# First phase of a gated expert block: each group of TensorE products is signalled by a Drain behind it in place of its last product

## The reference, cut to what matters

```
cf = sigmoid(fft2(n).real.mean(pixels) @ W.T + b)      # one factor per image and channel
sf = fft2(n.mean(channels)).real                       # one factor per image and pixel
x  = x + n * cf + n * sf                               # first half: "x1"
t  = tokens of x                                       # 16384 tokens of 64 channels
g  = layernorm(t) ; p = softmax(g @ gate_w + gate_b)   # 8 experts
e  = argmax(p) ; rank = running count of tokens sent to e
y  = (relu(g @ w1[e] + b1[e]) @ w2[e] + b2[e]) * p[e]  if rank < 2560 else 0
out = x + y, back as images
```

## Time and profile before

| | us |
|---|---|
| median of three executions | 496.19 |
| the profiled execution | 491.18 |
| its span | 488.8 |
| first phase, to the last indirect DMA of L445 | 0 to 262.6 |
| second phase | to 459 |

### The profile page before, as it was taken

The page is one execution under the profiler, slowest core; times in us unless marked ns, Lnnn a source line. Parts: engine busy times, 40 slices in busy tenths (PEclk is TensorE's granted clock), DMA queues, the critical chain, the costliest instruction groups (busy, mean ns, idle before and its releaser), DMA issues.

```text
span 488.8 us, 5544 instructions
## 1 busy us (share of the span) xinstructions
PE 278.9 (57%) x1574; PEld 197.2 (40%) x1574; DVE 248.2 (51%) x694; ACT 160.7 (33%) x301; POOL 227.0 (46%) x234
## 2 busy tenths in 40 slices
PE   7695645857191753614004888927477370839562
PEld 5584544846181653504001444514243130415251
DVE  4588366494554836645100367924445161527943
ACT  2362504342150513203000666714254051435300
POOL 0004727317366372757677335374726657461300
PEclk9666656576566665656555999986979586767967
DMA  7991010203000000000003513302113130100089
GB/s 242 413 380 49 29 51 26 60 7 97 11 11 13 4 15 5 15 12 12 13 14 79 105 28 69 82 24 66 44 29 72 40 68 24 34 19 4 7 312 375
DMA packets 38056, 36.16 MB, mean 74 GB/s; under 512 B 27995, under 2 KB 30620, under 8 KB 38034
## 3 DMA queue, kind: packets, MB, share of 16 engines
q1 hardware_dynamic: 29474, 25.71, 17.3%
q0 software_dynamic: 7264, 5.87, 4.2%
q10 hardware_dynamic: 1296, 4.33, 2.2%
HBM read 16.23 MB, written 21.36 MB: 77 GB/s over the span
## 4 chain that ended last, share of the span: by engine, by line
PE 31%; another core or an unknown queue 22%; DVE 18%; issue 12%; ACT 7%; POOL 4%; DMA 3%; SPq 1%; POOLq 0%; ACTq 0%; DVEq 0%
PE psD L1128 8%; PE psX L1115 4%; POOL slot_rows L445 4%; PE psC L1115 4%; PE psT L1048 3%; PE psD L1054 3%; PE psD L1138 3%; DMA x_flat<-token_out 2%; ACT hid L609 2%; DVE x L814 2%; DVE squares L692 2%; DVE rows L754 2%; PE psM L1099 2%; PE psC L973 2%
## 5 line engine op out<-in xcount | busy, mean ns | idle before, releaser
L445 POOL DMA_INDIRECT slot_rows<-rows,slots x128 | 127.2, 994 | 134.4 <-DVE slots L837 96.4
L481 POOL DMA_INDIRECT token_out<-ys,meta x94 | 94.5, 1005 | 96.1 <-DVE ys L913 69.1
L893 DVE TENSOR_TENSOR with_b<-psD,b_all 128x256 f32<-128x256 f32 x40 | 16.9, 423 | 88.9 <-remote 68.7
L1048 PE MATMUL psT<-kc,x 128*128 128x128 f32 x64 | 17.9, 435 | 63.4 <-DVE x L814 57.8
L1138 PE MATMUL psD<-kc,yT 128*128 128x128 f32 x80 | 19.2, 326 | 60.5 <-ACT yT L621 57.4
L1128 PE MATMUL psD<-hid,w_in 128*64 128x256 f32 x320 | 48.8, 431 | 2.1 <-ACT hid L609 2.1
L1138 PEld LDWEIGHTS psD<-kc,yT 128*128 128x128 f32 x80 | 8.6, 150 | 76.4 <-ACT yT L621 64.4
L1048 PEld LDWEIGHTS psT<-kc,x 128*128 128x128 f32 x64 | 11.5, 217 | 68.0 <-DVE x L814 59.2
L609 ACT ACTIVATE hid<-psC,b_in 128x512 f32<-128x512 f32 x40 | 25.5, 692 | 25.3 <-remote 11.0
L609 ACT ACTIVATE hid<-psX,b_in 128x512 f32<-128x512 f32 x40 | 25.4, 690 | 19.9 <-PE psX L1115 7.3
L621 ACT COPY yT<-psD 128x256 f32<-128x256 f32 x40 | 15.0, 374 | 49.9 <-remote 38.0
(11 more groups left out here) (155 smaller groups left out, 534.4 us busy)
## 6 DMA issues: line engine op xcount, KB each, us to landing
slot_rows<-empty_row SPq DMA_DIRECT2D x8, 660.0 KB, 8.1
slot_in<-slot_rows SPq DMA_DIRECT2D x7, 660.0 KB
x_in<-in_x_dram SPq DMA_DIRECT2D x8, 512.0 KB, 3.8
token_out<-zero_row SPq DMA_DIRECT2D x8, 512.0 KB, 10.9
slot_rows<-rows,slots POOLq DMA_INDIRECT x128
w_in<-in_L_ffn_w_dram SPq DMA_DIRECT2D x24, 64.0 KB
token_out<-ys,meta POOLq DMA_INDIRECT x94
x_in<-token_out SPq DMA_DIRECT2D x2, 512.0 KB, 4.0
```

Source lines behind the costliest of these rows:

```text
L445: pool.indirect_dma_start(out=slot_rows, out_offset=bass.IndirectOffsetOnAxis(ap=slots[G.u][:, s:s + 1], axis=0), in_=rows[G.u][:, s, :], ...
L481: pool.indirect_dma_start(out=token_out, out_offset=bass.IndirectOffsetOnAxis(ap=ids[:, UT * b + i, 1:2], axis=0), in_=ys[b][:, i, :], in_ ...
L893: nc.vector.tensor_tensor(with_b2[:], psD[:, 512 * w + 2 * P:512 * w + 2 * P + UT * C].rearrange("p (i c) -> p i c", c=C), b2_all[:, bass. ...
L1048: last = nc.tensor.transpose(psT[:, a * P:(a + 1) * P], x1[:, 2 * t:2 * t + 2, :].rearrange("p s c -> p (s c)"), ident)
```

## The change

In the first phase no product carries a signal any more. Behind the last product of each group TensorE gets a Drain instruction, and the Drain carries the increment. The order of the products, all waits, and the other engines' programs stay as they are. There are 13 such places in a middle turn and 104 in all. The four products of the set-up (L1078 to L1081) and all of the second and third phase keep their signals on the products.

```diff
                 for t in range(half * TT // 2, (half + 1) * TT // 2):
-                    last = nc.tensor.matmul(psC[:, t * P:(t + 1) * P], pixels(G)[:, t, :], centre,
-                                            start=True, stop=True)
+                    nc.tensor.matmul(psC[:, t * P:(t + 1) * P], pixels(G)[:, t, :], centre,
+                                     start=True, stop=True)
                 if half == 1:
-                    last.then_inc(x_centred, 1)
+                    nc.tensor.drain().then_inc(x_centred, 1)
...
-                    last = nc.tensor.transpose(psX[:, t * P:(t + 1) * P], pixels(G)[:, t, :], ident)
-                last.then_inc(x_turned, 1)
+                    nc.tensor.transpose(psX[:, t * P:(t + 1) * P], pixels(G)[:, t, :], ident)
+                nc.tensor.drain().then_inc(x_turned, 1)
...
-                    nc.tensor.matmul(p_sum, ones_b[:], counts[:, E:], start=False, stop=True).then_inc(base_mm, 1)
+                    nc.tensor.matmul(p_sum, ones_b[:], counts[:, E:], start=False, stop=True)
+                    nc.tensor.drain().then_inc(base_mm, 1)
...
-                    last.then_inc(logits_mm, 1)
+                    nc.tensor.drain().then_inc(logits_mm, 1)
...
-                    last.then_inc(cf_mm, 1)
+                    nc.tensor.drain().then_inc(cf_mm, 1)
...
-                        last.then_inc(x1_turned, 1)
+                        nc.tensor.drain().then_inc(x1_turned, 1)
...
-                        last.then_inc(x1_centred, 1)
+                        nc.tensor.drain().then_inc(x1_centred, 1)
```

More of the change, by code:

```diff
@@ L1002, in a_turn @@
                     nc.tensor.matmul(p_freq, mean_q[:].rearrange("p q s -> p (q s)"), dft_rows,
-                                     start=True, stop=True).then_inc(freq_mm, 1)
+                                     start=True, stop=True)
+                    nc.tensor.drain().then_inc(freq_mm, 1)
                     pe.wait_ge(xn_done, i + 1)
@@ L1007, in a_turn @@
                     for h in range(2):
-                        last = nc.tensor.matmul(p_col[:, h:h + 1], xn[0:1, h, :], ones[0:1, 0:1], start=True, stop=True)
-                    last.then_inc(col_mm, 1)
+                        nc.tensor.matmul(p_col[:, h:h + 1], xn[0:1, h, :], ones[0:1, 0:1], start=True, stop=True)
+                    nc.tensor.drain().then_inc(col_mm, 1)
                     pe.wait_ge(freq_done, i + 1)
@@ L1013, in a_turn @@
                     for a in range(2):
-                        last = nc.tensor.matmul(p_sf, row_freq[:, a * P:(a + 1) * P], dft_cols[:, a, :],
+                        nc.tensor.matmul(p_sf, row_freq[:, a * P:(a + 1) * P], dft_cols[:, a, :],
                                                 start=(a == 0), stop=(a == 1))
-                    last.then_inc(sf_mm, 1)
-                    nc.tensor.matmul(p_z, cwT[:], col[:], start=True, stop=True).then_inc(z_mm, 1)
+                    nc.tensor.drain().then_inc(sf_mm, 1)
+                    nc.tensor.matmul(p_z, cwT[:], col[:], start=True, stop=True)
+                    nc.tensor.drain().then_inc(z_mm, 1)
                 if T.back:
@@ L1021, in a_turn @@
                     for t in range(TT):
-                        last = nc.tensor.matmul(p_log[:, t * 2 * E:(t + 1) * 2 * E], x1T[:, t * P:(t + 1) * P], cgw[:],
+                        nc.tensor.matmul(p_log[:, t * 2 * E:(t + 1) * 2 * E], x1T[:, t * P:(t + 1) * P], cgw[:],
                                                 start=True, stop=True)
-                    last.then_inc(logits_mm, 1)
+                    nc.tensor.drain().then_inc(logits_mm, 1)
                 if T.front:
@@ L1028, in a_turn @@
                     for h in range(2):
-                        last = nc.tensor.matmul(p_cf[:, h * C:(h + 1) * C], colb[:, h, :], ident[0:C, 0:C],
+                        nc.tensor.matmul(p_cf[:, h * C:(h + 1) * C], colb[:, h, :], ident[0:C, 0:C],
                                                 start=True, stop=True)
-                    last.then_inc(cf_mm, 1)
+                    nc.tensor.drain().then_inc(cf_mm, 1)
                 if T.ahead:
@@ L1047, in turn_half @@
                             t = half * TT // 2 + a
-                            last = nc.tensor.transpose(psT[:, a * P:(a + 1) * P],
+                            nc.tensor.transpose(psT[:, a * P:(a + 1) * P],
                                                        x1[:, 2 * t:2 * t + 2, :].rearrange("p s c -> p (s c)"), ident)
-                        last.then_inc(x1_turned, 1)
+                        nc.tensor.drain().then_inc(x1_turned, 1)
                     def centre_half(half):
                         for t in range(half * TT // 2, (half + 1) * TT // 2):
-                            last = nc.tensor.matmul(psD[:, t * P:(t + 1) * P], x1T[:, t * P:(t + 1) * P], centre,
+                            nc.tensor.matmul(psD[:, t * P:(t + 1) * P], x1T[:, t * P:(t + 1) * P], centre,
                                                     start=True, stop=True)
-                        last.then_inc(x1_centred, 1)
+                        nc.tensor.drain().then_inc(x1_centred, 1)
                     turn_half(0)
```

## The result

The changed kernel takes **508.17 us** (median of four, 506.55 to 515.68) against 495.79 us for the kernel before (median of four, beside it): 1.026 times as long, 95% interval 1.019 to 1.034. Timed twice more, on two chips of the same kind, it was 514.24 against 493.23 us (1.046, 1.035 to 1.057) and 499.71 against 492.25 us (1.018, 1.009 to 1.028). It is slower; 448 us was forecast. Medians here are over all executions, while ratios and intervals compare only executions in the faster of two states, so they differ a little from the ratio of the medians. The profiled execution took 508.91 us with a span of 506.8 us, 18.0 us more than before. Its last indirect DMA of the first phase starts at 276.62 us in place of 261.66, so 15.0 of the 18.0 us arise in the first phase.

The account below looks back on a forecast made before the run. Late TensorE signals beside GpSimd's indirect DMAs were taken to bound the first phase. 491.2 us less 48.6 gained (Drains included) gives 442.6, plus 5.0 from profiled execution to median: 448 us; range 442 to 514.

Parts of the forecast that it names:

- the sum: First phase: on-time signals and Drains give turns of 20.6 us, GpSimd then bounds; gain 48.6 us, 442.6 us profiled.
- Removed: the increments on products: First-phase turn with every TensorE signal on time: 19.2 us in place of 29.3, before Drains are added.
- The argument that the array had done the work: Turn 6: full clock from 178.7 to 182.0 us directly behind L973 and L981, half clock after, signals still missing.
- rival B: TensorE stands at each Drain until late completion reports, from L1029 to L981: 512 us, up to 540; chance 0.20.
- five products running with three signals outstanding: Counted against TensorE being held at Drains: L993's products run at 178.79 us in turn 6 of the earlier trace.
- the head of the turn: Start of a turn, with the Drains of `x1_turned` and `x1_centred`, twice each; 0.8 us of Drains a turn.
- the side that had 0.35: Outcome slower by over 1%: half of Rival A and all of rival B, chance 0.35.
- Rival A: The Drain's increment is as late as the product's, first phase; only Drains are added: 496 to 511 us; chance 0.32.
- The Drain's price: First phase: 0.2 us for each Drain on a turn's path, seven of them, 1.4 us a turn.
- the sum's upper bound: First phase with Drains at 0.43 us each: turn of 22.2 us, the engines' chain bounds, 454 us.

Follow-up runs that it names:

- one DMA: Kernel before with one indirect DMA a group in place of sixteen in the first phase, most rows not sent: 411.23 us.
- plain ones: Kernel before with sixteen plain GpSimd DMAs a group in place of indirect ones, first phase: 423.03 against 493.23 us on S2, 379.5 against 405.68 on F1.
- S2: One of the five chips used for the follow-up runs; the kernel before takes 493.23 us there.
- F1: One of the five chips used for the follow-up runs; the kernel before takes 405.68 us there.
- bare Drains: Kernel before with every increment left on its product and a Drain without signal behind each of the 13 places: 516.35 against 498.67 us.
- F2: One of the five chips used for the follow-up runs; the kernel before takes 405.25 us there.
- one pause: Kernel before; GpSimd waits behind each group's eighth indirect DMA until all eight have landed: 486.53 against 493.23 us on S2, 415.56 against 405.68 on F1.
- S3: One of the five chips used for the follow-up runs; the kernel before takes 492.25 us there.

## Why the prediction was wrong

**The reading of what bounds the kernel was right**: late TensorE signals beside GpSimd's indirect DMAs. With one DMA the turn is 18.3 to 19.4 us (19.2 was worked out) and 87 us go; with plain ones 70.2 us go on S2. Part of that is GpSimd's own time, which falls too: on F1, where no signal is late, the same edit saves 26.2 us. That leaves 44 us for the lateness in the first phase by estimate, near the 48.6 us of the sum.

**The step that failed** is the first of the change: "Removed: the increments on products", with "L758 then starts at once and not at 175.75". It took a Drain to be punctual where a product's increment is late. The runs showed the Drain as late as the increment: in the changed kernel L758 starts at 187.68, 4.2 us behind its products' end, as it did before (4.2 us), and TensorE stands there too. The bare Drains show the same hold (22.2 and 17.5 us) without a signal of their own, so taking the increments away removes nothing. The argument that the array had done the work (the clock of 1.00 in the earlier trace rows) may be right and did not help: the Drain is not let go when the products' rows end. By the Trainium skill (PSUM — Partial Sum Buffer, Engine vs sequencer instructions) a drain "waits for the engine to go fully idle"; the held TensorE of the bare Drains (22.2 us ahead of L1037) agrees. Whether the results stand in PSUM early and only the report is late, no run here shows; nothing was read ahead of its signal.

**What happened is rival B** (0.20), in the place it was given and near the size in all. Worked out were 1.9 us a turn from L981 coming behind L973's release and 16 us in all, 512 us; measured are 2.0 us in turn 6, 14.5 us over turns 2 to 7, and 508, 514 and 500 us in three timings. The sum's agreement is in part luck: in turn 6 all 2.0 us come from L981 and nothing from the head of the turn, where 0.8 us was added, and the other turns grew by 1.4 to 3.9 us. What was counted against it, five products running with three signals outstanding, is no evidence: in the kernel before TensorE ran on with reports outstanding, and stood only once Drains were there. 508 us lies inside the range (442 to 514) and on the side that had 0.35.

**Rival A** gives nearly the same time, and the readers' waits of 3 to 5 us in turns of 29 to 31 us, its mark, are there too. The marks of B beside them decide: TensorE's own idle time ahead of L1032, L973 and L981 (22.7, 18.9 and 5.0 us).

**The Drain's price** was 0.2 us, and each gap is that. What the sum lacked is the lower clock that goes with the gaps: 3.6 us a turn in place of 1.4. Had the signals come on time, the turn would have been 22 us by this estimate and not 20.6: the price of the sum's upper bound (22.2), with its 454 us rather than 448.

**What the forecast could not hold**: on F1 and F2 the same kernel takes 405 us, and no trace from there has a late signal in either phase. A kernel before with the first phase on time and the second late would take some 449 us on S2 by estimate (493.23 less the 44 us above), so the 448 us fits what on-time signals would have given there. No rows of one execution could tell that there are two cases.

Open stay: why the reports are late on three chips and not on two others; why they come in a few steps (in turn 6 at 10.1, 17.2 and 22.9 us behind the burst's start, before and after the change alike); and whether the products complete late or only their reports travel late.

## What to carry to other kernels

A Drain behind a group does not speed a late signal up: it is let go as late and makes TensorE wait as well, so an increment on the product is the better place, above all where work of the engine follows. Ask of a late signal what else runs when it is late, and change that (here the form of GpSimd's DMAs, or pauses between them), not the messenger. Before tuning against such a lateness, time the kernel on more than one chip: one pause gained 2.0% on S2 and cost 2.4% on F1.

## What the hardware showed unexpectedly

- The same kernel took 492 to 499 us (medians; single runs 486 to 500) on three chips and 405.3 and 405.7 us (404 to 408) on two. Beside indirect DMAs TensorE's signals of turn 6 are 4 to 12 us behind the products' modelled ends in the first trace, and on F1 0.03 to 0.04 us in turn 5.
- Sixteen plain DMAs of GpSimd took it 0.54 us each and held up no signal on S2. Eight indirect ones, 0.97 us each, in a burst as long held the logits' signal for 2.9 us there.
- The last reports of a turn came 3.6 to 3.7 us behind the start of a full burst's last indirect DMA, and in a pause of GpSimd (turn 5 on S3) 2.5 us behind it.
- Gaps of 0.2 us behind thirteen Drains a turn went with a mean granted clock of 0.62 in place of 0.70, and with 375 ns in place of 307 for a MATMUL of the logits (48 of them in three turns).
